# A graph-network kernel whose last layer normalises late: one final normalisation in two parts, transposes of the maxima behind the weighted products, value remainders on GpSimd

## The reference

```python
H_l = H @ W_l; H_r = H @ W_r
S = H_l @ H_r.T                       # 4096 x 4096
beta = softmax(S, axis=-1)
O = beta @ H @ W_h @ W_g
x = layernorm(H + adj @ H + gamma * O)   # eps 1e-5, the output
```

## Time and profile before

| | us |
|---|---|
| median of 3 runs (1305.02 to 1307.64) | 1307.47 |
| the profiled execution's own time | 1307.26 |
| its span | 1305.4 |
| PE busy | 1259.0 (96%) |
| DVE busy | 958.2 (73%) |
| ACT busy | 800.9 (61%) |
| POOL busy | 233.7 (18%) |
| mean granted TensorE clock | 0.993 |

### The profile page before, as it was taken

One profiled execution on the slowest core, in us unless ns is written; L12 is line 12 of the kernel. 1 busy time (PEld: TensorE's weight loads), 2 busy tenths in 40 slices (PEclk: granted clock), 3 DMA queues, 4 the chain that ended last, 5 costly groups with the idle time before them and its releaser, 6 DMA issues.

```text
span 1305.4 us, 17888 instructions
## 1 busy us (share of the span) xinstructions
PE 1259.0 (96%) x6139; PEld 829.7 (64%) x6139; DVE 958.2 (73%) x1265; ACT 800.9 (61%) x966; POOL 233.7 (18%) x136
## 2 busy tenths in 40 slices
PE   8999999989999899999999999999999999999987
PEld 3566666643332334788888888886677776767764
DVE  7987987720000556899999898978878888878885
ACT  1334555511110224788888777867978778788795
POOL 0100000000000000001010000012334333354355
PEclk9999999989999899999999999999999999999999
DMA  9877766589999699999999999960000000000000
GB/s 366 317 272 295 288 238 241 206 334 354 359 344 409 251 390 388 311 369 386 371 379 367 366 352 382 363 248 1 1 1 1 1 1 1 1 19 15 1 1 32
DMA packets 82816, 294.33 MB, mean 225 GB/s; under 512 B 9658, under 2 KB 11322, under 8 KB 82746
## 3 DMA queue, kind: packets, MB, share of 16 engines
q1 hardware_dynamic: 80496, 292.59, 59.7%
q10 hardware_dynamic: 2250, 0.82, 0.2%
HBM read 291.27 MB, written 2.10 MB: 225 GB/s over the span
## 4 chain that ended last, share of the span: by engine, by line
PE 85%; DVE 6%; DMA 4%; ACT 3%; issue 2%; DVEq 0%; SPq 0%; ACTq 0%
PE acc L1612 9%; PE acc L1607 9%; PE acc L1608 9%; PE acc L1694 8%; PE acc L1546 8%; DMA raw<-in_adj_s 4%; PE acc L1460 4%; PE acc L1452 3%; PE acc L1456 3%; PE acc L1453 3%; PE acc L1684 2%; PE acc L1688 2%; PE acc L1685 2%; PE rs L1469 2%; PE e L1649 2%; PE rs L1651 2%
## 5 line engine op out<-in xcount | busy, mean ns | idle before, releaser
L1161 DVE TENSOR_TENSOR t_lo<-raw,t_hi 128x1024 fp32r<-128x1024 f32 x256 | 303.2, 1230 | 21.6 <-ACT t_hi L847 18.2
L847 ACT ACTIVATE t_hi<-raw 128x1024 fp32r<-128x1024 f32 x256 | 261.5, 1054 | 38.0 <-PE acc L1612 36.9
L1607 PE MATMUL acc<-t_hi,st_hi 128*128 128x512 f32 x512 | 201.9, 394 | 0.6 <-ACT t_hi L847 0.6
L1608 PE MATMUL acc<-t_hi,st_lo 128*128 128x512 f32 x512 | 199.6, 390 | 0.0
L682 POOL TENSOR_TENSOR ring_lo<-ring,p_hi 128x1024 fp32r<-128x1024 f32 x64 | 155.4, 2429 | 231.3 <-ACT p_hi L897 231.2
L1612 PE MATMUL acc<-t_lo,st_hi 128*128 128x512 f32 x512 | 158.9, 392 | 1.4 <-DVE t_lo L1161 1.1
L1246 DVE TENSOR_TENSOR ring<-ring,e 128x1024 f32<-128x1024 f32 x128 | 153.9, 1210 | 0.1
L891 ACT ACTIVATE ring<-ring 128x1024 f32<-128x1024 f32 x128 | 134.2, 1054 | 23.1 <-DVE ring L1246 22.6
L637 POOL COPY xb<-x 128x512 f32<-128x512 f32 (+1 forms) x24 | 32.3, 1345 | 588.5 <-DVE xs L1079 214.8
L1694 PE MATMUL acc<-ring,x 128*128 128x512 f32 x256 | 120.4, 592 | 0.0
L1612 PEld LDWEIGHTS acc<-t_lo,st_hi 128*128 128x128 f32 x512 | 95.0, 188 | 24.6 <-DVE t_lo L1161 4.8
(11 more groups left out here) (228 smaller groups left out, 2181.2 us busy)
## 6 DMA issues: line engine op xcount, KB each, us to landing
raw<-in_adj_s SPq DMA_DIRECT2D x518, 512.0 KB, 5.6
kept_t<-in_adj_s SPq DMA_DIRECT2D x8, 512.0 KB, 7.2
x<-in_x SPq DMA_DIRECT2D x4, 512.0 KB, 9.2
kept_l<-in_adj_s SPq DMA_DIRECT2D x4, 512.0 KB, 7.3
kept_s<-in_adj_s SPq DMA_DIRECT2D x4, 512.0 KB, 6.5
kept_v<-in_adj_s SPq DMA_DIRECT2D x4, 512.0 KB, 6.6
kept_e<-in_adj_s SPq DMA_DIRECT2D x4, 512.0 KB, 8.5
kept_late<-in_adj_s SPq DMA_DIRECT2D x4, 512.0 KB, 11.1
```

The costliest lines, as they stand in the source:

```text
L847: nc.scalar.activation(t_hi[:, g % HL, :], raw[:, k, :], ACT.Copy).then_inc(hi_done, 1)
L1161: nc.vector.tensor_tensor(t_lo[:, k, :], raw[:, slot_no(s, c, g), :], t_hi[:, k, :].bitcast(F32), ALU.subtract).then_inc(lo_done, 1)
L1607: mm(a[:, :], block_of(st_h, b), hi[:, m], start=(g == 0 and j == 0), stop=False)
L1608: mm(a[:, :], block_of(st_l, b), hi[:, m], start=False, stop=False)
```

## The change

Four edits.

1. The final normalisation is in two parts, blocks 0 to 27 and 28 to 31. Nothing of it stands in the tick loops any more. Behind its last tick ScalarE takes the root of the first part, normalises blocks 0 to 5, *then* evacuates the last row's weighted sum (L909 before), and then normalises blocks 20 to 27; VectorE normalises blocks 6 to 19 before the last row's finish. The second part is shared two and two. GpSimd normalises nothing.
2. On TensorE `weighted(t - 21)` comes before `transpose_peak` and before `peak_row` of its tick.
3. On VectorE `maximum(t)` comes before `diagonal`.
4. `values_lo` (eight instructions) is on GpSimd, ahead of its first `weights_lo`.

```diff
-        LN_PARTS = ((0, 16), (16, 24), (24, NB))
-        LN_SCALES = (NT - 34, NT - 4)
-        POOL_LN = {NT - 53: (0, 3), ... NT - 9: (22, 24)}
-        LN_LAST = (NB - 2 * CB, NB - 3, NB)
+        LN_PARTS = ((0, NB - CB), (NB - CB, NB))
+        ACT_FIRST, DVE_FIRST, ACT_SECOND = (0, 6), (6, 20), (20, NB - CB)
+        DVE_LAST, ACT_LAST = (NB - CB, NB - 2), (NB - 2, NB)
+        RESULT = (ACT_FIRST + ("fin_xa", 1), DVE_FIRST + ("fin_x", 1), ACT_SECOND + ("fin_xa", 2),
+                  DVE_LAST + ("fin_x", 2), ACT_LAST + ("fin_xa", 3))
...
 # GpSimd
-            def normalise_first(a, b):
...
+            def values_lo(j):
+                k = SPLIT[j]
+                pool.wait_ge(vh_done, j + 1)
+                nc.gpsimd.tensor_tensor(v_lo[:, j, :], x[:, 2 * k * D:2 * (k + 1) * D],
+                                        v_hi[:, j, :].bitcast(F32), ALU.subtract).then_inc(vl_done, 1)
...
+            for j in range(min(NSPLIT, 9)):
+                values_lo(j)
             for n in range(NT):
                 if n % KP in SPLIT:
                     weights_lo(n)
-                if n in POOL_LN:
-                    normalise_first(*POOL_LN[n])
...
 # ScalarE, tick and behind the ticks
-                if t in LN_SCALES:
-                    last_deviation(LN_SCALES.index(t))
             ticks(tick)
+            last_deviation(0)
+            last_norm(0, *ACT_FIRST)
             evacuate_weighted(GQ - 1)
-            last_deviation(2)
-            last_norm(*LN_LAST[1:])
+            last_norm(0, *ACT_SECOND)
+            last_deviation(1)
+            last_norm(1, *ACT_LAST)
...
 # VectorE
+                if t < NT:
+                    maximum(t)
                 if t % KP == 0 and 0 < t <= NT:
                     diagonal(t // KP - 1)
-                if t < NT:
-                    maximum(t)
...
-                if 12 <= t < 12 + NSPLIT:
-                    values_lo(t - 12)
...
-                if t + 1 in LN_SCALES:
-                    last_variance(LN_SCALES.index(t + 1))
-                if t - 1 in LN_SCALES:
-                    last_scales(LN_SCALES.index(t - 1))
             ticks(tick)
+            last_variance(0)
+            last_scales(0)
+            last_norm(*DVE_FIRST)
             finish_sums(GQ - 1)
             finish_add(GQ - 1)
             finish_stats(GQ - 1)
-            last_variance(2)
-            last_scales(2)
-            last_norm(*LN_LAST[:2])
+            last_variance(1)
+            last_scales(1)
+            last_norm(*DVE_LAST)
...
 # TensorE
+                if 0 <= t - LAG < NT:
+                    weighted(t - LAG)
                 if t % KP == 0 and 0 < t <= NT:
                     transpose_peak(t // KP - 1)
                 if t % KP == 1 and 1 < t <= NT + 1:
                     peak_row(t // KP - 1)
-                if 0 <= t - LAG < NT:
-                    weighted(t - LAG)
```

More of the change, by code:

```diff
@@ L332, in build @@
          bt_done, out_mm, lrec_done, lg_done, o1_done, o2_done, sa_done, mva_done, fin_ve,
-         fin_std, fin_rc, fin_nmr, fin_x, fin_xa, fin_xp, l_mm) = (sem(n) for n in (
+         fin_std, fin_rc, fin_nmr, fin_x, fin_xa, l_mm) = (sem(n) for n in (
             "wt_mm wt_done wt_mean wt_scaled wt_centred qk_mm qk_done q_mm q_hi_done "
@@ L337, in build @@
             "bt_done out_mm lrec_done lg_done o1_done o2_done sa_done mva_done fin_ve "
-            "fin_std fin_rc fin_nmr fin_x fin_xa fin_xp l_mm").split())
+            "fin_std fin_rc fin_nmr fin_x fin_xa l_mm").split())
         def cols(t, c, width=CW):
@@ L496, in build @@
         S4_PREPARED = {0: 2, 1: 1, 14: 0}
-        LN_PARTS = ((0, 16), (16, 24), (24, NB))
-        LN_SCALES = (NT - 34, NT - 4)
-        POOL_LN = {NT - 53: (0, 3), NT - 51: (3, 6), NT - 49: (6, 9), NT - 47: (9, 12), NT - 45: (12, 14), NT - 43: (14, 16),
-                   NT - 15: (16, 18), NT - 13: (18, 20), NT - 11: (20, 22), NT - 9: (22, 24)}
-        LN_LAST = (NB - 2 * CB, NB - 3, NB)
-        RESULT = ((0, 9, "fin_xp", 1), (9, 16, "fin_xp", 2), (16, 24, "fin_xp", 3), LN_LAST[:2] + ("fin_x", 1),
-                  LN_LAST[1:] + ("fin_xa", 1))
+        LN_PARTS = ((0, NB - CB), (NB - CB, NB))
[3 more added lines that the diff above has]
+                  DVE_LAST + ("fin_x", 2), ACT_LAST + ("fin_xa", 3))
         def score_bank(t):
@@ L605, in _ @@
             for a, b, by, count in RESULT:
-                sp.wait_ge({"fin_x": fin_x, "fin_xa": fin_xa, "fin_xp": fin_xp}[by], count)
+                sp.wait_ge({"fin_x": fin_x, "fin_xa": fin_xa}[by], count)
                 sp.dma_start(out[:, a * D:b * D], v[:, a * D:b * D]).then_inc(out_done, 16)
@@ L688, in _ @@
                 add_one(j)
+            for j in range(min(NSPLIT, 9)):
+                values_lo(j)
             for n in range(NT):
+                if 9 <= n + 7 < NSPLIT:
+                    values_lo(n + 7)
                 if n % KP in SPLIT:
                     weights_lo(n)
-                if n in POOL_LN:
-                    normalise_first(*POOL_LN[n])
         @block.scalar
@@ L914, in last_deviation, with last_norm @@
                 nc.scalar.activation(std_a[:, a:b], ve_a[:, a:b], ACT.Sqrt).then_inc(fin_std, 1)
-            def last_norm(a, b):
-                act.wait_ge(fin_nmr, 3)
+            def last_norm(part, a, b):
+                act.wait_ge(fin_nmr, part + 1)
                 for n in range(a, b):
@@ L1207, in _ @@
             chunks(dve, step)
[L1209 to L1213, removed]
             def maximum(t):
```

## The result

| | before | changed |
|---|---|---|
| median, first comparison | 1307.41 (4 runs) | 1297.73 (4 runs, 1295.24 to 1299.54) |
| ratio | | 0.9931, 95% interval 0.9914 to 0.9948 |
| profiled execution's own time | 1307.26 | 1299.54 |
| its span | 1305.4 | 1297.6 |
| from the first copy of the maxima to the span's end | 423.8 | 415.1 |

The forecast was 1300.6 with a range of 1298.8 to 1304.5. The direction was right and the gain too small: 6.8 us against 9.7 by the medians, which lies under the range. On two other chips the changed kernel came out at ratios of 0.9917 (0.9897 to 0.9937) and 0.9928 (0.9908 to 0.9947).

A forecast was written before the change was run, and what follows sets the result against it. TensorE was taken to bound the kernel, with time to gain only where it waits. 1307.26 - 2.5 - 1.55 - 1.0 - 0.9 - 0.8 = 1300.5, set to 1300.6 for the median; 8-in-10 range 1298.8 to 1304.5.

The forecast's parts named there:

- the waits of the table loads: TensorE's fold at tick 96: its 2.50 us wait comes from ScalarE's table loads and goes, -2.5 us (bounds 0 and -2.5).
- GpSimd's remainder as what is late next: Behind tick 127: GpSimd's remainder ends at 1265.6, TensorE is there at 64.7, so 0.9 us is given back.
- the cover of the end: Between ScalarE's last `p_hi` and `bt`: 5.06 us that hides 4.6 us of load, root and six blocks; cost 0.
- the lock of VectorE against GpSimd: At the end, `nmr` waits for GpSimd's last remainder, moving from 1291.15 to 1291.8 and making `bt` 0.05 late; nothing added.
- tick 128: Last row's fold: the 2.49 us wait goes, 0.9 is given back, net -1.55 us (bounds -0.9 and -2.5).
- the transposes behind the product: Six row starts on TensorE: a product between scores and transposes saves 0.17 us each, -1.0 us (bounds 0 and -1.5).
- ticks 12 to 21: Before TensorE's tick 21: earlier copy of maxima 0.6, moved value remainders 0.3, together -0.9 us (bounds 0 and -2.7).
- the end: Last blocks and output DMA: fewer final blocks, landing stays 2.2 to 2.3 us, -0.8 us (bounds -0.3 and -1.0).
- Waits that belong to the row ends: Rival: row ends, not table loads, cause the waits at ticks 96 and 128; 1301.8 or 1305.6, together chance 0.12.
- Cover too thin: Rival at the end: `bt` waits for ScalarE's six blocks, price 0.6 to 2.4 us, so 1301.2 to 1303; chance 0.2.
- The late row: Slower rival: VectorE's first subtractions wait for the row of maxima at seven row starts, +12.2 us, 1312.8; chance 0.06.
- The gain that turns into waits later: Same-time rival: gains at ticks 96 and 128 become waits a few ticks later; sum 1306, chance 0.04.

The follow-up runs named there:

- edit 2 alone: Kernel before with only the weighted product moved ahead of the transposes and the row of maxima; ratio 0.9962.
- edit 1 alone: Kernel before with only the final normalisation in two parts behind the ticks, products and maxima ordered as before; ratio 0.9937.
- the run with the root at tick 126: Kernel before with its second root at tick 126 instead of 124; the last product comes 5.0 us later.
- six roots: Kernel before with four more roots of constants, at ticks 46, 62, 78 and 110; median 1326.96 against 1308.93, ratio 1.0126.
- the early load: Changed kernel with the exponential's table loaded in tick 0; medians 1298.75 (ratio 0.9919) and, repeated, 1298.73 (ratio 0.9923).
- mid-row root: Kernel before with first root and GpSimd's first normalisation part eight ticks later, root at tick 102; trace 1.6 us shorter up to tick 118.
- edits 3 and 4 alone: Kernel before with only the copy of the maxima ahead of the reduction and the value remainders on GpSimd; ratio 0.9989.
- the last run of the kernel before: Kernel before, unchanged, run once more for its trace; 425.2 us from the first copy of the maxima to the end.
- the kernel before again: Kernel before, unchanged, against itself; ratio 0.9998, trace 424.9 us from the first copy of the maxima to the end.

## Why the prediction was right or wrong

**Right: the mechanism and its places.** The bound (TensorE), the waits of the table loads, their disappearance, GpSimd's remainder as what is late next, the cover of the end and the lock of VectorE against GpSimd are in the trace where the record put them. Edit 1 and edit 2 alone show it: each shortens what it was said to. Only at tick 128 did the loads hold less than the record's "same wait" suggests, 0.9 of 2.49 us; the odd product filled the rest, as the record had stepped.

**Wrong: the waits were not all counted.** The step that failed is the statement that the whole price of the loads stands in one wait at each row's end, 2.50 at tick 96 and 2.49 at tick 128, and that only these two exist. At tick 126 there was a third of 1.11 us, worth about 1.4 between starts. The record shows the rows around tick 96, where nothing but the fold waits, and takes tick 124 to be the same, though the load stands two ticks further from its row's end. It was the largest single omission: with it the sum is 1299.2, inside the range. In edit 2 alone, which keeps the loads, this wait stays (1.11); in edit 1 alone it is gone.

**Wrong: a wait was priced at its own length.** At long waits TensorE's granted clock falls to half in some executions, which costs 1.2 us (tick 16) or 1.4 to 1.7 us (ticks 96 and 128), and 4.7 in the run with the root at tick 126, where it lasted 10 us. The one trace before the forecast had three waits of 1.94 to 2.50 us and no fall. Over the eighteen traces 12 of the 27 waits of 1.94 us and more, from the first copy to the last product, had one beside them, and no fall stands anywhere else in that stretch. At tick 16 three of nine waits of 1.94 or 1.95 us had one, and none of nine of 1.71 to 1.75 us, which the changed kernel has; that these shorter ones are safe is not shown by so few. The three traces of the kernel before average 424.63 us, the three of the changed kernel 415.17: 9.5 us, near what the medians give (9.7, 11.1, 9.5). So some 0.8 us of the gain are falls that no longer happen. That number rests on two falls in three traces; an estimate from all traces with the same waits (three falls of nine at tick 16, three of six at tick 96, two of six at tick 128) is 1.7 us. That falls cost time and stand at waits is shown by six roots.

**Mis-sized: the transposes behind the product.** 0.17 for each of six rows was forecast, 0.25 came, 1.5 us instead of 1.0; it is inside the bounds. The rest is not the slower first product behind the transposes, which the bound had named: that is still there (0.31 us to the next one, 0.32 before). It is the start of that product, 0.35 us behind the transposes where it was 0.41.

**Mis-sized: ticks 12 to 21.** 0.9 was forecast, 0.58 came. The step that gave the copy's 0.6 and the remainders' 0.3 as a sum is wrong, since both run against the same ScalarE, whose table load ends the gain; the early load moved what they could not.

**Mis-sized: the end.** 0.8 forecast, 1.3 measured, outside the bound of 1.0. The landing was taken as the same for every size from two rows of 192 and 320 KB; the last piece, now of 128 KB behind another of 128, lands 0.5 us sooner.

**Right within 0.2: tick 128.** 1.55 against 1.34. The fold came 0.14 later than stepped.

**The rivals.** Waits that belong to the row ends: no at tick 96 (mid-row root, edit 1 alone), in part at tick 128, where 1.61 of the 2.49 us stay without any load. Cover too thin: it held with 0.1 us, in part by luck. The record counted the root's 0.22 us twice (the 0.68 us of the earlier trace rows begin with the root's start) and wrote 1293.8 where its own terms make 1293.95; against that, root to first block took 1.21 us and not 0.68, by the offset's wait and a longer reciprocal. The late row: no. The gain that turns into waits later: no, apart from the 0.69 us counted beforehand. The Trainium skill's drain at a table switch ("ScalarE: Activation LUTs", "What ACT_TABLE_LOAD costs") does not show at the end either: the last `p_hi` ends at 1282.94, the load runs from 1282.96 to 1284.24, and the root starts at 1284.25. The Trainium skill's rule on two SBUF inputs ("SBUF — State Buffer", "Who interferes with whom") agrees with the 0.56 us of the offset, against 0.17 alone.

**The range** was too narrow on its low side. Its parts had bounds, but they were those of the terms that had been found; a term that was overlooked and a price that one trace happened not to show had none.

## What to carry to other kernels

Before a wait is priced by its neighbour, list every wait of the bounding engine in the whole stretch: the same stall lands on another instruction when it starts a few ticks further from the next meeting point. Work that sits on an engine with slack should stand far ahead of such a meeting point (ten ticks ahead a load cost 1.0 us, two or four ticks ahead 2.3 to 2.5), or outside the loop where another engine is still busy for longer than the work takes. Here a stall of 1.94 us or more on TensorE cost more than its length in 12 of 27 cases, so removing one gives back more on average than a trace without a fall shows.

## What was unexpected of the hardware

- The fall of the granted clock comes by chance: the same wait of 2.50 us at tick 96 had one in three of its traces (edits 3 and 4 alone, the last run of the kernel before, six roots) and none in three others (the first trace, the second root two ticks later, the kernel before again); an equal wait at tick 112 of six roots had none.
- A good part of the scatter from run to run has the same source. Summing one minus the granted clock over windows of 1 us, the sweeps lose 3.4, 5.1, 6.8 or 8.5 us of clock in the eighteen traces, steps of 1.7 us. With 3.4 the first copy of the maxima is at 877.6 to 879.9, with 8.5 at 883.0 to 884.4 (there both kernels are among them; those with 3.4 are all variants of the changed one). This is more than half of the gain under study, and only counting from a point behind the sweeps made terms of 0.3 us readable.
- The bracketed idle time of a TensorE row can be shorter than what the stall costs. At tick 126 the scores start 1.50 us behind the product ahead of them (1251.78 to 1253.28), where 0.23 is regular, and the next one follows after 0.31: 1.35 us in all, while the bracket says 1.11, because a product's row reaches past the start of the next. Before transposes the two agree: at tick 96 they start 2.88 us behind the last score product and at tick 48, without a wait, 0.40, which leaves 2.48 against a bracket of 2.50.
